# A comparison mask in a threshold search: built from POOL's scaled scores and one edge per row instead of ScalarE's array of signs

## What is computed

```
dots = einsum('bhid,bhjd->bhij', q, k) * QK_SCALE      # 16 heads, q and k normalized, 4 memory keys in front
dots = einsum('hg,bgij->bhij', W_pre_th, dots)         # heads mixed
dots = where(causal, mask_value, dots)
vk   = top_k(dots, 64)[0][..., -1:]                    # the 64th largest score of each row
dots = where(dots < vk, mask_value, dots)
attn = softmax(dots); attn = einsum('hg,bgij->bhij', W_post_th, attn); out = attn @ v ...
```

## Time and profile before

| | us |
|---|---|
| median of 3 runs | 3893.15 |
| lowest, highest run | 3878.56, 3899.26 |
| the profiled execution: its own time | 3893.2 |
| its span in the trace | 3891.4 |

### The profile page before, as it was taken

How to read it: one execution, slowest core, us unless ns; L and a number is a source line. 1 busy time by engine, 2 the same in 40 slices (tenths; PEclk the granted TensorE clock), 3 DMA queues, 4 the chain that set the end, 5 groups by cost and what they waited for, 6 DMA issues and landing times. The chain is left out here.

```text
span 3891.4 us, 73246 instructions
## 1 busy us (share of the span) xinstructions
PE 3344.1 (86%) x22950; PEld 2143.0 (55%) x22950; DVE 2820.0 (72%) x6363; ACT 2577.6 (66%) x5953; POOL 2402.7 (62%) x6033
## 2 busy tenths in 40 slices
PE   7999999995888998888888858888988888888798
PEld 4444444443555566655556635555666555566466
DVE  6667776763778888578888867788885788877354
ACT  3444444553778889578888837888895778888221
POOL 2666666664776667577666637766675766666232
PEclk9999999995889999889999968999997899999899
DMA  3222222224555553355555325555533555541110
GB/s 129 82 92 92 87 92 92 92 98 142 140 156 164 167 153 90 99 146 167 162 167 138 81 66 143 153 168 168 151 92 96 150 160 167 168 124 47 53 33 28
DMA packets 362425, 466.47 MB, mean 120 GB/s; under 512 B 29524, under 2 KB 294100, under 8 KB 361560
## 3 DMA queue, kind: packets, MB, share of 16 engines
q1 hardware_dynamic: 361944, 461.02, 40.3%
HBM read 226.57 MB, written 234.36 MB: 118 GB/s over the span
## 5 line engine op out<-in xcount | busy, mean ns | idle before, releaser
L1019 ACT ACTIVATE junk<-D,nt 128x76 int8<-128x76 f32 (+62 forms) x1440 | 1070.8, 746 | 182.8 <-POOL nt L1104 144.9
L931 PE MATMUL banks<-kr,E 128*128 128x128 f32 (+1 forms) x4672 | 736.7, 308 | 195.7 <-issue 96.0
L931 PEld LDWEIGHTS banks<-kr,E 128*128 128x128 f32 (+1 forms) x4672 | 629.6, 210 | 307.3 <-issue 283.9
L904 PE MATMUL banks<-Sg,kpre 128*128 128x109 f32 (+51 forms) x1568 | 647.4, 513 | 21.7 <-DVE D L1225 11.1
L1042 ACT ACTIVATE AT<-banks 128x512 f32<-128x512 f32 (+3 forms) x768 | 345.7, 479 | 330.5 <-PE banks L951 167.5
L890 PE MATMUL banks<-kT,qT 64*128 64x343 f32 (+11 forms) x896 | 403.3, 533 | 178.6 <-DVE Sn L1214 161.5
L1304 DVE SCALAR_TENSOR_TENSOR E<-D,vk,E 128x12 f32<-128x12 f32 (+56 forms) x512 | 378.7, 757 | 211.8 <-DVE vk L1260 133.9
L1214 DVE COPY Sn<-banks 128x686 f32<-128x686 f32 (+7 forms) x448 | 376.9, 841 | 141.4 <-PE banks L891 133.1
L1240 DVE SCALAR_TENSOR_TENSOR W<-SG,sgn,W 128x76 f32<-128x76 int8 (+14 forms) x480 | 413.8, 901 | 85.2 <-POOL W L1120 83.2
L546 DVE RECIPROCAL a_share<-a_share 128x512 f32<-128x512 f32 x128 | 419.9, 3324 | 70.5 <-POOL a_share L490 37.0
L951 PE MATMUL banks<-AT,V 128*64 128x64 f32 x9216 | 370.8, 233 | 64.1 <-issue 49.1
(11 more groups left out here) (188 smaller groups left out, 5815.2 us busy)
## 6 DMA issues: line engine op xcount, KB each, us to landing
score_scratch<-Sn SPq DMA_DIRECT2D x96, 343.0 KB, 3.3
q_scratch<-a_share SPq DMA_DIRECT2D x32, 512.0 KB, 2.7
v_scratch<-a_share SPq DMA_DIRECT2D x32, 512.0 KB, 3.7
k_scratch<-a_share SPq DMA_DIRECT2D x32, 512.0 KB, 2.7
gate_scratch<-a_share SPq DMA_DIRECT2D x32, 512.0 KB, 2.7
kT<-k_scratch SPq DMA_DIRECT2D x32, 512.0 KB, 4.7
qT<-q_scratch SPq DMA_DIRECT2D x32, 512.0 KB, 6.4
gateT<-gate_scratch SPq DMA_DIRECT2D x32, 512.0 KB, 12.0
```

What stands on the lines that cost most here:

```text
L904: out = nc.tensor.matmul(bank[:, 0:c], kpre[:].rearrange("p h r -> p (h r)"), Sg[:, g % 3, c0:c1], start=True, stop=not diagonal)
L931: out = nc.tensor.matmul(ps[5 + i % 2][0:rows, c % 4 * P:(c % 4 + 1) * P], E[:, g % 4, c * P:c * P + rows], kr[:, g % 4, :], start=True, s ...
L1019: nc.scalar.activation(out, D[:, e, 1:1 + n], ACT.Sign, bias=nt[:, r, e:e + 1], scale=-1.0, accum_out=cnt[:, r, e:e + 1]).then_inc(s[f"cnt ...
```

## The change

The mask of `sides` no longer comes from SG. POOL computes an edge per row, nt3 * sgn * -2^-50, that is, the guess put through the same two products as the scores in W; DVE compares W itself with that edge (greater than) and subtracts the result from W, so that W is both inputs and the output. The two products on 128 x 2 stood in `judge`, with the other sign, as tie 0 and tie 1; they now stand in `nearest` between sgn and W, under a new semaphore edge, and `judge` subtracts where it added. ACT's fourth count writes its signs into an array last that nobody reads, and waits for cnt3 of the pair before instead of for pick.

```diff
@@ count (ACT) @@
-                if r == 3:
-                    if i >= 2:
-                        act.wait_ge(s["pick"], i - 1)
-                    out = SG[:, g % 2, 0:n]
-                else:
-                    if r == 0 and i >= 2:
-                        act.wait_ge(s["cnt2"], i - 1)
-                    out = junk[:, g % 2, 0:n]
+                if r == 0 and i >= 2:
+                    act.wait_ge(s["cnt2"], i - 1)
+                if r == 3 and i >= 2:
+                    act.wait_ge(s["cnt3"], i - 1)
+                out = (last if r == 3 else junk)[:, g % 2, 0:n]
@@ nearest (POOL) @@
                 ts(sgn[:, e], off[:, e], -1.0, 1.0, ALU.max, ALU.min).then_inc(s["side"], 1)
                 pool.wait_ge(s["side"], FP[p] + 1)
+                chain(tt(edge[:, 0, e], nt[:, 3, e], sgn[:, e], ALU.mult))
+                ts(edge[:, 1, e], edge[:, 0, e], -SMALL, None, ALU.mult).then_inc(s["edge"], 1)
                 pool.wait_ge(s["prob"], 2 * p - 2)
@@ judge (POOL) @@
                 pool.wait_ge(s["pos"], FP[p] + 1)
-                chain(tt(tie[:, 0, e], nt[:, 3, e], sgn[:, e], ALU.mult))
-                chain(ts(tie[:, 1, e], tie[:, 0, e], SMALL, None, ALU.mult))
+                pool.wait_ge(s["edge"], FP[p] + 1)
                 ts(far[:, e], pos[:, e], 15.5, None, ALU.is_gt)
                 pool.wait_ge(s["pick"], 2 * FP[p] + 2)
-                chain(tt(tie[:, 2, e], m8[:, e, 0], tie[:, 1, e], ALU.add))
-                chain(ts(tie[:, 3, e], tie[:, 2, e], 0.0, None, ALU.is_equal))
-                tt(bad[:, e], tie[:, 3, e], far[:, e], ALU.add).then_inc(s["bad"], 1)
+                chain(tt(tie[:, 0, e], m8[:, e, 0], edge[:, 1, e], ALU.subtract))
+                chain(ts(tie[:, 1, e], tie[:, 0, e], 0.0, None, ALU.is_equal))
+                tt(bad[:, e], tie[:, 1, e], far[:, e], ALU.add).then_inc(s["bad"], 1)
@@ sides (DVE) @@
+                    dve.wait_ge(s["edge"], FP[p] + 1)
                     dve.wait_ge(s["v"], i + 1)
-                    nc.vector.scalar_tensor_tensor(out=W[:, h, 0:n], in0=SG[:, h, 0:n], scalar=sgn[:, e:e + 1],
-                                                   in1=W[:, h, 0:n], op0=ALU.is_equal, op1=ALU.subtract,
+                    nc.vector.scalar_tensor_tensor(out=W[:, h, 0:n], in0=W[:, h, 0:n], scalar=edge[:, 1, e:e + 1],
+                                                   in1=W[:, h, 0:n], op0=ALU.is_gt, op1=ALU.subtract,
                                                    reverse1=True).then_inc(s["near"], 1)
```

More of the change, by code:

```diff
@@ L682 @@
                 x_st=1, s_ps=1, s_sb=1, s_st=2, sg_in=3, mixed=1, taken=1, near=1, best=1, nt0=1, nt1=1, nt2=1, nt3=1, cnt0=1,
-                cnt1=1, cnt2=1, cnt3=1, side=1, pos=1, base1=1, base2=1, base3=1, v=1, pick=1, vk=1, bad=1, flag=1, exp=1, e_zero=1, prob=1, rinv=1, kr=1,
+                cnt1=1, cnt2=1, cnt3=1, side=1, pos=1, edge=1, base1=1, base2=1, base3=1, v=1, pick=1, vk=1, bad=1, flag=1, exp=1, e_zero=1, prob=1, rinv=1, kr=1,
                 post=1, at=1, av=1, ut=1, y=1, x_ok=1, link=1, chain=1, general=1)
@@ L732, in attention @@
         D = sb("D", [P, 8, KW])
-        SG = sb("SG", [P, 2, JW], I8)
+        last = sb("last", [P, 2, JW], I8)
+        edge = sb("edge", [P, 2, 8])
         junk = sb("junk", [P, 2, JW], I8)
@@ L768, in attention @@
         vk = sb("vk", [P, 8])
-        tie = sb("tie", [P, 4, 8])
+        tie = sb("tie", [P, 2, 8])
         far = sb("far", [P, 8])
```

## The result

The changed kernel takes 3897.91 us, the median of 20 runs (3882.81 to 3919.79). The kernel before takes 3884.97 us in 20 runs beside it (3877.31 to 3899.26). The ratio is 1.0033, with a 95% interval of 1.0022 to 1.0044: 13 us slower (9 to 17). The prediction had +11 us. Its 3904.0 stands on the three runs shown before, whose median of 3893.15 turned out to lie 8 us above that of the 20, so the difference is the number to compare. The profiled execution of the changed kernel took 3898.14 us (span 3896.3).

A forecast was written before the change was run, and what follows sets the result against it. No engine was full (PE busy 86%); waits handed round a ring between the engines were taken to bound the kernel. From 3893.2 us, 0 + 11 + 0 gave 3904 us, range 3883 to 3927.

The forecast's parts named there:

- Part 1: ACT's fourth count no longer waits for pick: at most 72.7 us at stake, costed at 0.
- The rival that the removed wait pays: ACT starts the counts behind the fourth earlier: 52 us at most, 17 if a third arrives, 3876 us; chance 0.07.
- Part 2: POOL's two products move from judge to between sgn and W: W starts 0.52 us later, costed at +11 us.
- Kind (b): Pairs where POOL waits for pick in judge: W waits for older selections anyway (47 times, 74.5 us), mostly costing nothing.
- Kind (a): Pairs where POOL runs without idling from judge to off: 0.60 us gained at judge, 0.52 given back before W, net zero.
- Kind (c): Pairs where POOL waits at off for ACT's fourth count: 65 x 0.52 = 34 us at most, 77/240 arriving, 11 us.
- The rival that the delay goes round the ring: Each step adds its 0.52 us to the next through ACT's wait for nt: 34 us, 3927 or more; chance 0.15.
- Part 3: DVE's comparison in sides reads f32 and f32, one tile twice, instead of int8 and f32: costed at 0.
- The rival of half speed: DVE's 480 instructions with W twice grow by up to 0.75 us: 360 us, a third giving 4013; chance 0.02.

The follow-up runs named there:

- the repetition: The changed kernel measured once more without any edit, against the kernel before: 3896.36 us, ratio 1.0045.

## Why the prediction was right, and where only its number was

**Part 1, the removed wait, at 0: right, by the mechanism named.** The held step of the earlier trace rows in the changed kernel:

```profile
1083.58 0.60 ACT L1017 ACTIVATE last<-D,nt 128x380 int8<-128x380 f32 x1
...
1087.07 0.19 POOL L1130 TENSOR_TENSOR tie<-m,edge 128x2 f32<-128x2 f32 x1 [3.77 <-DVE hit L1256]
...
1088.21 0.49 ACT L1040 ACTIVATE AT<-banks 128x384 f32<-128x384 f32 x1 [3.34 <-PE banks L952]
```

The count starts 3.49 us ahead of tie, not 0.14, and AT idles 3.34 us for PE instead of 0.68. Over the span, 72.7 us left the wait for pick and 41 came up at AT; putting the wait back moved 50.3 the other way. The rival that the removed wait pays is refuted by that run.

**Part 2, the 0.52 us: right.** The wide step has 0.47 more from sgn to W (0.79 beside 0.32), and L1240 idles 0.53 longer. The second product was not stretched there: 0.23. The stretch to 1 us each, which the prediction held possible, was small in the mean as well: 257 and 286 ns for the two, beside 204 and 235 in judge.

**Kind (b), hidden by W's own waiting: right, and more often than counted.** In the page of the kernel before the group of W reads

```profile
L1120 POOL TENSOR_SCALAR W<-D,sgn 128x76 f32<-128x76 f32 (+14 forms) x480 | 344.6, 728 | 111.7 <-issue 74.5
```

POOL's idle time in front of W fell from these 111.7 us to 24.9; another 19.9 + 21.0 us of hand-over stand in front of the two products. Pair by pair the two traces show it directly. In 76 of the 240 pairs W had idled 0.15 us or more, and in those it starts no later behind sgn than before. In the other 164 it starts 0.50 us later on average. The prediction had 47 pairs of this kind.

**Kind (a), net zero: not shown.** It was argued that 0.60 gained in judge pays for 0.52 lost ahead of W. Judge's gain alone is worth nothing (1.0005). The 164 pairs in which W stands 0.50 us further behind sgn are about as many as kinds (a) and (c) have together (105 and 65), but that judge's gain offsets the delay in most of them is only suggested, by the second pair of products at 0.30 us a pair against 0.05 to 0.07 for the first.

**Kind (c), a third of 34 us arrives: right number, but the wrong engine for the share.** The step took DVE's waits for W, 77 of 240, as the share of pairs in which the delay reaches the end. But DVE's late start was not needed for the loss: with W in time and ACT's guess late the ratio is 1.0066, and with W and DVE late and the guess back in time it is 1.0002. The waits that belong to this path are ACT's for the guess, 219 in all rounds. The trace of the kernel before tells how many of them stand behind W: 156, for 112.5 us, and 167 for 168.4 us after the change. Of the 65 pairs in which POOL waited at off, DVE then waited for W in 30 and ACT for the guess in 50. Neither share is a third, and how many of these waits reach the end of the kernel was not counted. So 11 beside 13 (and beside 17 in the repetition) is partly luck.

All traces together, with starts counted from off, as means over the searched pairs (for the guess those that have a next pair), in us. L1240 stands for the same instruction of each kernel:

| kernel | next guess | L1240 | ratio |
|---|---|---|---|
| before, pos behind the guess | 3.31 | 2.67 | 0.9996 |
| before, pos and products behind the guess | 3.31 | 2.69 | 0.9983 |
| one product ahead of W, pos behind | 3.39 | 2.75 | 0.9966 |
| changed, pos behind the guess | 3.63 | 2.93 | 1.0002 |
| edge on DVE | 3.67 | 2.87 | 1.0043 |
| before | 3.74 | 2.63 | 1 |
| before, no products in judge | 3.75 | 2.70 | 1.0005 |
| one product ahead of W | 3.87 | 2.78 | 0.9985 |
| only the products moved | 4.02 | 2.83 | 1.0052 |
| wait for pick put back | 4.07 | 2.87 | 1.0026 |
| changed | 4.09 | 2.87 | 1.0033 |
| products behind W | 4.23 | 2.59 | 1.0066 |
| products twice | 4.63 | 3.18 | 1.0222 |

With a guess up to 0.13 us later than before there is no loss, except with the edge on DVE; from 0.28 us on there always is. The start of L1240 doesn't sort the kernels in this way.

**The rival that the delay goes round the ring** names the right engines (ACT, POOL's nt, ACT), and its price of 34 us was too high: 13 us were measured, 17 in the repetition and 20 with the products alone moved. The reason given against it fits the trace (at AT ACT waits for PE 59 times for 208.6 us), but no run tested it alone.

**Part 3, the operands, at 0: right.** The groups that answer to the earlier trace rows:

```profile
L1240 DVE SCALAR_TENSOR_TENSOR W<-W,edge 128x972 f32<-128x972 f32 x1 | 2.0, 1977 | 2.1 <-POOL W L1120 2.1
...
L1240 DVE SCALAR_TENSOR_TENSOR W<-W,edge 128x956 f32<-128x956 f32 x1 | 1.2, 1210 | 0.0
```

1210 ns beside 1212 with int8. The rival of half speed is refuted. Its 0.75 us an instruction isn't derived (901 ns doubled would be 0.90 more), but nothing hangs on it. The Trainium skill, page "Vector Engine (DVE) Microarchitecture Reference", section "Points that are easy to get wrong", has this instruction at half throughput with two non-bf16 SBUF sources. An int8 source is not bf16 either, so that sentence gives no reason for a difference between the two kernels, and none is there: int8 with f32, and f32 with f32 out of one tile, take the same time. No run here has a bf16 source.

**What was missing from the step** is the work that stands between W and the next guess. pos and move are each stretched to about 1 us by L1240, and moving pos, which only hit and judge read, behind the guess repays the whole loss.

## What to carry to other kernels

- Ahead of a move on a queue, list every instruction behind it and its reader, and price the reader that works in a ring with this queue, not the one that waits most visibly. Here DVE waited for W in plain sight, and it was ACT's next guess, a few instructions further on, whose delay cost time.
- The size of an engine's wait is not what shortening it brings: 37 us more of one wait came with a loss of 13 us, 46 us less of the same wait with nothing in one kernel, and 43 us less with a gain of 13 us in another.
- A wait that is taken away must be looked for in the next one of the same engine before it is counted as a gain.

## What the runs showed of the hardware

**Small POOL operations are stretched beside a DVE operation with two SBUF inputs, and which one is hit depends on the order.** The groups of POOL, changed kernel, then the products behind W, then the changed kernel with pos behind the guess:

```profile
L1122 POOL TENSOR_TENSOR pos<-off,sgn 128x2 f32<-128x2 f32 x240 | 110.9, 462 | 0.0
...
L1113 POOL TENSOR_TENSOR edge<-nt,sgn 128x2 f32<-128x2 f32 x240 | 61.7, 257 | 19.9
```

```profile
L1124 POOL TENSOR_TENSOR edge<-nt,sgn 128x2 f32<-128x2 f32 x240 | 125.0, 521 | 0.0
```

```profile
L1125 POOL TENSOR_TENSOR pos<-off,sgn 128x2 f32<-128x2 f32 x240 | 60.9, 254 | 0.0
```

The same product has a mean of 257 ns ahead of W, while DVE often waits, and 521 behind it, where L1242 (the L1240 of that kernel) often runs; pos goes from 462 to 254 when it leaves that place. The stretch does not vanish with it but goes to the operation that follows: with pos gone, the mean of nt rises from 312 to 400 ns, and in the wide step move and nt take 0.99 and 0.96 us, where pos and move took 0.99 and 1.07. In the wide step each of these ends within 0.1 us of the end of one of the two L1240.

**The time of one and the same kernel goes with its granted clock from run to run.** Among 29 runs of the kernel before on one chip the fastest took 3873.41 us at a mean clock of 0.924 and the slowest 3902.01 at 0.912; a line through all of them falls 1.7 us for each 0.001 of clock. For the fastest kernel here it is 3861.4 at 0.927 and 3892.86 at 0.915. Whether a slower clock lengthens the span or a longer span, with more idling of PE, comes with a lower clock, these runs don't tell. The spread of one kernel, 0.7%, is thus twice the loss that is at issue here, and the loss shows only in medians of several runs. It is also a reason why the run with the edge on DVE stays open.
